# Expert up product with the weights as the stationary side, in a fused audio-tower block on one core

## The reference

```
scores = sigmoid(xf @ gate_w.T);  top_scores, top_idx = top_k(scores, 2)
buf[e, pos] = token                      # 64 experts, tokens sorted into slots
h = silu(buf @ w1[e]) * (buf @ w3[e])    # w1, w3: 128 x 64 for each expert
y = h @ w2[e]                            # w2: 64 x 128
out = shared(xf) + sum of the token's two y, each times its score + residual
```

## Time and profile before

| | |
|---|---|
| median of 3 runs | 320.98 us |
| profiled execution, its time | 321.12 us |
| profiled execution, its span | 319.3 us |
| TensorE: matmul records, busy | 2106, 197.5 us |
| VectorE busy | 214.1 us |
| GpSimd busy | 171.8 us |
| ScalarE busy | 61.9 us |
| granted TensorE clock, mean | 0.804 of 2.4 GHz |

### The profile page before, as it was taken

One profiled execution on the slowest core, in us unless ns is written; L12 is line 12 of the kernel. 1 busy time (PEld: TensorE's weight loads), 2 busy tenths in 40 slices (PEclk: granted clock), 3 DMA queues, 4 the chain that ended last, 5 costly groups with the idle time before them and its releaser, 6 DMA issues.

```text
span 319.3 us, 5301 instructions
## 1 busy us (share of the span) xinstructions
PE 197.5 (62%) x2106; PEld 159.1 (50%) x2106; DVE 214.1 (67%) x427; ACT 61.9 (19%) x167; POOL 171.8 (54%) x120
## 2 busy tenths in 40 slices
PE   0062828996767793894793694567277848989300
PEld 0052727874555573673582484442246727877200
DVE  0023986769899769989789859957839663374152
ACT  0033000020110110020020011011224752635300
POOL 2245776598669639669368676525205332003771
PEclk9999996999996859796598579755556796999755
DMA  8999999999953916565899100097810020824422
GB/s 280 241 383 364 418 423 418 417 418 418 397 200 113 359 56 233 213 232 205 268 218 225 49 0 20 25 200 211 225 38 10 8 66 18 233 68 117 115 62 72
DMA packets 32866, 64.14 MB, mean 201 GB/s; under 512 B 2858, under 2 KB 25351, under 8 KB 32391
## 3 DMA queue, kind: packets, MB, share of 16 engines
q1 hardware_dynamic: 30138, 59.17, 56.0%
q0 software_dynamic: 1024, 2.10, 2.3%
q10 hardware_dynamic: 1678, 2.52, 2.2%
HBM read 55.91 MB, written 7.86 MB: 200 GB/s over the span
## 4 chain that ended last, share of the span: by engine, by line
DVE 40%; PE 23%; DMA 15%; issue 8%; POOL 7%; ACT 3%; SPq 1%; POOLq 1%; DVEq 0%
PE bank L649 7%; DVE ring L957 7%; DMA mask<-in_L_tok_mask_dram 7%; DVE sc L987 6%; DMA ring<-in_L_tok_weight_dram 6%; DVE o L1000 5%; DVE prod L977 3%; POOL ring L453 3%; DVE prod L997 3%; DVE sc L979 3%; POOL rstd L373 2%; PE bank L690 2%; PE bank L780 2%; PE bank L805 2%; PE bank L790 2%
## 5 line engine op out<-in xcount | busy, mean ns | idle before, releaser
L384 POOL TENSOR_TENSOR ring<-ring,mask 128x896 f32<-128x896 f32 x48 | 104.9, 2202 | 22.4 <-DMA ring<-in_L_tok_weight_dram 22.2
L649 PE MATMUL bank<-ring,xT 128*64 128x128 f32 x1248 | 92.5, 312 | 39.5 <-POOL ring L384 27.5
L649 PEld LDWEIGHTS bank<-ring,xT 128*64 128x64 f32 x1248 | 82.9, 160 | 46.0 <-POOL ring L384 29.6
L957 DVE TENSOR_TENSOR ring<-ring,bank 128x1024 f32<-128x1024 f32 x24 | 29.1, 1214 | 31.2 <-ACT bank L474 18.3
L373 POOL TENSOR_TENSOR rstd<-mv,half 128x1 f32<-128x1 f32 (+1 forms) x24 | 18.3, 762 | 46.7 <-DVE mv L966 46.5
L404 POOL DMA_INDIRECT expert_inputs<-xf,scatter_index x16 | 21.8, 1365 | 35.0 <-DVE scatter_index L1065 32.6
L453 POOL DMA_INDIRECT ring<-expert_outputs,gather_index x16 | 16.0, 1000 | 26.8 <-DMA expert_outputs<-ring 22.2
L957 DVE TENSOR_TENSOR ring<-ring,mask 128x512 f32<-128x512 f32 x24 | 24.9, 1038 | 0.0
L987 DVE TENSOR_TENSOR sc<-sc,mx 128x16 f32<-128x16 f32 (+7 forms) x8 | 21.1, 2638 | 0.3
L1133 DVE TENSOR_TENSOR mask<-ring,bank 32x256 f32<-32x256 f32 (+1 forms) x24 | 10.0, 418 | 11.5 <-ACT ring L560 11.3
L780 PE MATMUL bank<-w,ring 128*64 128x128 f32 (+1 forms) x256 | 15.7, 305 | 1.5 <-DVE ring L1124 1.5
(11 more groups left out here) (137 smaller groups left out, 305.3 us busy)
## 6 DMA issues: line engine op xcount, KB each, us to landing
ring<-in_L_tok_weight_dram SPq DMA_DIRECT2D x48, 832.0 KB, 9.6
ring<-expert_inputs SPq DMA_DIRECT2D x6, 512.0 KB, 5.8
expert_outputs<-ring SPq DMA_DIRECT2D x12, 256.0 KB, 3.0
mask<-in_L_tok_mask_dram SPq DMA_DIRECT2D x3, 832.0 KB, 16.3
expert_inputs<-prod ACTq DMA_DIRECT2D x2, 1024.0 KB, 11.4
w2p<-in_L_ffn_w_dram SPq DMA_DIRECT2D x2, 1024.0 KB, 10.5
w<-in_x_dram SPq DMA_DIRECT2D x1, 1250.0 KB, 13.8
expert_inputs<-ring SPq DMA_DIRECT2D x1, 1024.0 KB, 12.5
```

Of the source, the lines that this page charges most:

```text
L384: pool.tensor_tensor(unit(j, q, SPLIT, UC), unit(j, q, SPLIT, UC), mask[:, (m + SPLIT) * D:(m + UC) * D], ALU.mult).then_inc(s_pmask, 1)
L649: last = pe.matmul(bank[j % 2][64 * par:64 * par + 64, 0:D], xT[:, (UC * t + c) * B:(UC * t + c + 1) * B], unit(j, 2 * t + par, c, c + 1), ...
L957: dve.tensor_tensor(both(j, t, a, b), both(j, t, a, b), m.rearrange("p (u f) -> p u f", u=1).to_broadcast([P, 2, (b - a) * D]), ALU.mult). ...
```

## The change

`up` swaps its sides. For each expert and each of `w1` and `w3` one matmul has the weight (128x64) as the stationary side and streams the expert's 64 or 32 slots. The result lies with the middle's 64 columns on the partitions: even experts on partitions 0 to 63, odd ones on 64 to 127, the slots along the free axis, `w1`'s product in columns 0 to 255 of the bank and `w3`'s in 256 to 511. That is the form in which `down` needs it. So `turn_mid`, `copy_midT`, the block-shaped tiles, their zeroing (four GpSimd memsets) and ScalarE's 0/1 multiplications (L558) are gone. `mid` is one 128x256 product on either engine. `down` now does one expert in a matmul, with 64 rows of the middle (partitions 0 to 63 or 64 to 127) against that expert's 64 rows of `w2`. The step of TensorE becomes `up(g)`, `turn_xs(g+2)`, `down(g-1)`, that of ScalarE `silu(g)`, `copy_y(g-1)`, `copy_xsT(g+2)`, and there is one step fewer. `down` writes to banks 7 and 3 in turn in all groups, where it used bank 7 alone for groups 0 to 7.

```diff
 def silu(g):                                  # ScalarE
     ...
     if g < STEPS_C:
-        for par in range(2):
-            act.activation(gt[g % 2][:, :, H * par:H * par + H], both[:, :, H:2 * H], ACT.Identity,
-                           scale=cst[:, C_PAR + par:C_PAR + par + 1])
-    act.activation(sil[g % 2], both[:, :, 0:H], ACT.Silu).then_inc(s_sil, 1)
+        act.copy(linear[g % 2], bank[U_BANK(g)][:, 256:512])
+    act.activation(gated[g % 2], bank[U_BANK(g)][:, 0:256], ACT.Silu).then_inc(s_sil, 1)
-def copy_midT(g):
     ...
 def up(g):                                    # TensorE
     ...
-    for l in range(count):
-        row, tile = l * slots % P, l * slots // P
-        last = pe.matmul(bank[U_BANK(g)][row:row + slots, tile * P:(tile + 1) * P],
-                         xsT[g % 2][:, l * slots:(l + 1) * slots],
-                         w13[:, first + l].rearrange("p a h -> p (a h)"), start=True, stop=True)
+    for n in range(count // 2):
+        for a in range(2):
+            for par in range(2):
+                l = 2 * n + par
+                last = pe.matmul(bank[U_BANK(g)][64 * par:64 * par + H, 256 * a + n * slots:256 * a + (n + 1) * slots],
+                                 w13[:, first + l, a], xsT[g % 2][:, l * slots:(l + 1) * slots], start=True, stop=True)
-def turn_mid(g):
     ...
 def down(g):
-    pe.wait_ge(s_hT, g + 1)
+    pe.wait_ge(s_hm, g + 1)
     ...
-    if g >= 1:
-        pe.wait_ge(s_ys, g if g <= GROUPS1 else g - 1)
-    if g == GROUPS1 + 1:
-        pe.wait_ge(s_flag, 1)
-    for n in range(count // 2):
-        row, tile = 2 * n * slots % P, 2 * n * slots // P
-        last = pe.matmul(bank[Y_BANK(g)][row:row + 2 * slots, tile * D:(tile + 1) * D],
-                         hT[g % 2][:, 2 * n * slots:2 * (n + 1) * slots], w2p[:, first // 2 + n, :],
-                         start=True, stop=True)
+    if g >= 2:
+        pe.wait_ge(s_ys, g - 1)
+    for l in range(count):
+        n, par = l // 2, l % 2
+        row, tile = l * slots % P, l * slots // P
+        last = pe.matmul(bank[Y_BANK(g)][row:row + slots, tile * D:(tile + 1) * D],
+                         midT[g % 2][64 * par:64 * par + H, n * slots:(n + 1) * slots],
+                         w2p[64 * par:64 * par + H, first // 2 + n, :], start=True, stop=True)
 def expert_steps(first, last):
     ...
             up(g)
-        if 1 <= g <= GROUPS:
-            turn_mid(g - 1)
-        if g >= 2:
-            down(g - 2)
         if g + 2 < GROUPS:
             turn_xs(g + 2)
+        if 1 <= g <= GROUPS:
+            down(g - 1)
 def mid(g):                                   # VectorE
-    for r in range(P // slots):
-        rows, half = slice(slots * r, slots * (r + 1)), r % 2 * H
-        last = dve.tensor_tensor(hm[MID_TILE(g)][rows, :, half:half + H], sil[g % 2][rows],
-                                 bank[U_BANK(g)][rows].rearrange("p (i f) -> p i f", f=2 * H)[:, :, H:2 * H], ALU.mult)
-    last.then_inc(s_hm, 1)
+    dve.tensor_tensor(midT[g % 2], gated[g % 2], bank[U_BANK(g)][:, 256:512], ALU.mult).then_inc(s_hm, 1)
 # GpSimd
-for i in range(4):
-    pool.memset(hm[2 + i], 0.0).then_inc(s_hmz, 1)
```

More of the change, by code:

```diff
@@ L200, in tower_kernel @@
         xsT = [ring_view(14336 + 512 * i, 512) for i in range(2)]
-        hT = [ring_view(15360 + 512 * i, 512) for i in range(2)]
-        sil = [ring_view(16384 + 256 * i, 256).rearrange("p (i h) -> p i h", h=H) for i in range(2)]
+        gated = [ring_view(15360 + 256 * i, 256) for i in range(2)]
+        linear = [ring_view(15872 + 256 * i, 256) for i in range(2)]
+        midT = [ring_view(16384 + 256 * i, 256) for i in range(2)]
         sw13 = ring_view(16896, 2 * D).rearrange("p (a d) -> p a d", a=2)
@@ L261, in tower_kernel @@
                                                  sem("shared_down"), sem("shared_added"))
[L262 to L265, removed]
+        s_t1, s_xsT, s_m1, s_sil, s_hm, s_m2, s_ys = (
+            sem("xs_transposed"), sem("xsT_copied"), sem("up"), sem("silu"), sem("mid"), sem("down"), sem("y_copied"))
         s_yout = [sem("y_out_1"), sem("y_out_2")]
@@ L425, in mid @@
                 if g >= 2:
[L426 to L429, removed]
+                    pool.wait_ge(s_m2, g - 1)
+                pool.tensor_tensor(midT[g % 2], gated[g % 2], linear[g % 2], ALU.mult).then_inc(s_hm, 1)
             pool.wait_ge(s_tok, 3 * NCH)
@@ L607, in _ @@
             copy_xfT(NCH - 1)
-            expert_steps(STEPS_C, GROUPS + 2)
+            expert_steps(STEPS_C, GROUPS + 1)
             silu_shared(1)
@@ L777, in up @@
                     pe.wait_ge(s_hm, g - 1)
-                for l in range(count):
-                    row, tile = l * slots % P, l * slots // P
-                    last = pe.matmul(bank[U_BANK(g)][row:row + slots, tile * P:(tile + 1) * P],
-                                     xsT[g % 2][:, l * slots:(l + 1) * slots],
-                                     w13[:, first + l].rearrange("p a h -> p (a h)"), start=True, stop=True)
-                last.then_inc(s_m1, 1)
-            def turn_mid(g):
-                pe.wait_ge(s_hm, g + 1)
-                if g >= 2:
-                    pe.wait_ge(s_hT, g - 1)
-                for i in range(PG):
-                    last = pe.transpose(bank[M_BANK(g)][:, i * P:(i + 1) * P], hm[MID_TILE(g)][:, i, :], ident)
-                last.then_inc(s_t2, 1)
+                for n in range(count // 2):
[4 more added lines that the diff above has]
+                                             w13[:, first + l, a], xsT[g % 2][:, l * slots:(l + 1) * slots], start=True, stop=True)
@@ L1166, in _ @@
             gather_slots(1, NCH1, NCH)
-            dve.wait_ge(s_hmz, 4)
             dve.wait_ge(s_hm, STEPS_C)
```

22 lines of the change are left out of this document (4 added, 18 removed).

## The result

The changed kernel took 330.0 us (328.2 to 332.1, 4 runs) against 321.5 (317.7 to 322.3, 4 runs): ratio 1.033, 95% interval 1.027 to 1.039. Slower, where 317.7 us was forecast. That is the result on record, but not all of it: run again untouched in later batches, on two chips, the same kernel took 316.8 and 315.8 us, 0.6% **less** than the kernel before.

The account below looks back on a forecast made before the run. Two paths end close together: group 7's store with the gathers (3.7 to 5.0 us earlier), and the shared expert with eight combines, ending last, 3.4 us earlier: 321.12 - 3.4 = 317.7 us; range 316 to 319.5, 8 in 10 314.7 to 322.

Parts of the forecast that it names:

- second path: Table 2's products, shared expert and eight combines: products end at 293.1, last combine 3.4 us earlier; this path ends last.
- What follows is unchanged: From the end of the products on, nothing changes: first combine at 306.0, last one at 310.6 instead of 314.06.
- Rival one: Gain dies at the end: hand-overs from TensorE some 3 us late beside gathers, 320.7 or 323.7 us; chance 0.24.
- (a): Around the last chunk's exponential: narrower GpSimd product, slots' transposes already done, ScalarE's table load earlier; -0.75 us.
- (b): Step 4, 4.7 us at a clock of 0.60: the 0.25 us saved per step counts as -0.4 us.
- (c): Steps 5 to 7 of TensorE: 0.25 us less each, -0.75 us together.
- (d): From step 8's up product to the copy of group 7's result: down product one step sooner, 3.7 against 5.52, -1.8 us.
- The store of group 7: Store behind group 7's copy took 4.29 us where the median is 3.0: up to 1.3 us more gain, by luck.
- rival four: More comes through: lateness gone, GpSimd's path ends last, clock may give another 1 us; 315 us, chance 0.10.
- GpSimd's path: Group 7's copy and store, then 16 gathers 1.30 us apart: ends 3.7 to 5.0 us earlier.
- Rivals two and three: Two: down product's row halves do not run together, 333 us, chance 0.08. Three: weight loads bind, 328 us, chance 0.04.

Follow-up runs that it names:

- before_again: The kernel before, run again untouched on chip C: 317.8 us.
- after_again: The changed kernel, run again untouched on chip C: 316.8 us, ratio 0.994 to the kernel before.
- b_plain: The kernel before plus 12 plain transfers of 128 rows from ScalarE's queue, three a step in steps 4 to 7, chip A: 318.3 us.
- held12: The changed kernel with GpSimd's gathers also waiting for the last group's down product, chip A: 324.2 us, ratio 1.013 to the kernel before.
- up12: The changed kernel with GpSimd's gathers waiting for the 12th (last group's) up product, chip B: 322.2 us, ratio 1.011 to the kernel before.

## Why the prediction was wrong

**The step that failed** is in the second path: "steps 8 and 9 take 3.6 each, step 10 3.0 ... 293.1", with every instruction of table 2 at its undisturbed rate beside gathers that now start 3.9 us earlier. In the first pair these parts took until 311.8, and the second path did not win 3.4 us but lost 8.5 (last combine 322.51 against 314.06). What failed is thus an overlap taken as free. In its place the runs show TensorE held back from 289.6 to 305.1 beside the gathers, and at the lower clock until 311.8; why it is held back stays open.

**Another error in the same path hid part of that.** "What follows is unchanged" kept the 12.9 us between the end of the products and the first combine (294.83 to 307.74), and the late signals of before are in these. Behind the stall it is 6.2 us (311.78 to 317.96), and 6.1 us on chip C (292.96 to 299.08). So the products ended 18.7 us after the forecast's 293.1, and the last combine only 11.9 us after its 310.6.

**Rival one had the place and not the size.** I had seen the lateness in the earlier trace rows and priced it as a delay of 3 us for each hand-over in the last group, 320.7 to 323.7 us, chance 0.24. It was the edge of something that holds back the instructions themselves. In the kernel before only the end of TensorE's work lay under the gathers, and the last combine waited for the last gather all the same: on chip C, without the lateness, it waits 1.87 us for it, against 1.68. From the scatter of the last chunk but one to the last combine it is 71.36 us with the lateness (242.70 to 314.06) and 71.23 without (239.67 to 310.90); the two traces' other difference, 3.0 us, lies ahead of that scatter. So the lateness cost the kernel before next to nothing, and its price could not be read there. The changed kernel starts its gathers with two `up` and three `down` products to go, and the 13th gather waits for them. An estimate of the worst was missing: a stall lasting as long as table 1's gathers, 12 x 1.30 = 15.6 us, laid on the path that I had forecast to end last, gives 317.7 + 15.6 = 333 us. That number could have been written down. It is no strict bound: the gaps last 15.5 us, but from `up` of group 10 to the end of the products it is 24.2 us against 7.1 on chip C, 17.1 more, and 2.6 of them lie behind the gaps, at the lower clock.

**How the sum stands without the stall.** On chip C both kernels were profiled, and the steps can be held against each other, in us at fixed points of before and after:

| point | before_again | after_again | difference |
|---|---|---|---|
| scatter of the last chunk but one | 239.67 | 240.00 | +0.33 |
| exponential's table load | 247.21 | 247.44 | +0.23 |
| `up` of group 4 | 262.08 | 262.20 | +0.12 |
| `up` of group 5 | 267.34 | 267.06 | -0.28 |
| `up` of group 8 | 277.76 | 278.71 | +0.95 |
| copy of group 7's result | 283.29 | 282.42 | -0.87 |
| first gather | 288.53 | 286.18 | -2.35 |
| last combine | 310.90 | 308.38 | -2.52 |

The lines that the readings below rest on, three of after_again, then one of before_again:

```profile
267.06 1.63 PE L754 MATMUL bank<-ring,w 128*64 128x64 f32 x32
...
272.70 0.66 PE L738 MATMUL bank<-cst,ring 128*128 128x128 f32 x4 [1.32 <-DMA ring<-expert_inputs]
...
308.38 0.35 DVE L1139 SCALAR_TENSOR_TENSOR ring<-ring,wts,hres 128x128 f32<-128x128 f32 x1 [1.85 <-DMA ring<-expert_outputs,gather_index]
...
310.90 0.35 DVE L1183 SCALAR_TENSOR_TENSOR ring<-ring,wts,hres 128x128 f32<-128x128 f32 x1 [1.87 <-DMA ring<-expert_outputs,gather_index]
```

- (a), the exponential, -0.75 forecast: -0.21 at `up` of group 4, counted from the scatter. Wrong in this pair. In the first pair the table load did come 0.8 us earlier against the scatter (247.94 - 240.49 = 7.45 against 250.97 - 242.70 = 8.27), but before_again has 7.54: what I read in the earlier trace rows was mostly that execution's own.
- (b), step 4, -0.4: -0.40. Right.
- (c), steps 5 to 7, -0.75: +1.23. Wrong, and this is a further step that failed. In step 6 the slots' transposes wait 1.32 us for the load of group 8's slots, which is chained to the last scatter; they stood behind `down` before, and the change puts them ahead of it, so a late load holds `down` as well. I had moved them in the sum and not asked what they wait for. Another 0.48 us went to a stretch partly at the lower clock in step 5 (`up` 1.63 us instead of 1.15, granted 0.67). Without the two it is -0.57.
- (d), -1.8: 282.42 - 278.71 = 3.71 against 283.29 - 277.76 = 5.53, so -1.82. Right.
- The store of group 7, "up to 1.3 more, as luck has it": from the copy's end to the first gather 3.17 us against 4.65, 1.5 less. The first pair has 3.16 against 5.17, so it was no luck; why it lands sooner was not tested.
- Which path ends last: GpSimd's, in both kernels, by 1.85 and 1.87 us of the last combine's wait. I had the second path last; rival four, GpSimd's path at 315 us, has it right and chips B and C agree with it (315.8, 316.8). That 317.7 lies near these too is luck: it was added up along a path that does not end last, with 6.7 us of late signals in it that these runs do not have.

**Rivals two and three are refuted on every chip.** Two halves of the array's rows run together: 16 records of `down` take 1.09 us, 0.06 us each, where one after another was to be 1.8. (That rival's price is also too high as added up: its 0.87 and 2.6 us a group are counted from the 0.89 of before, where the forecast has 1.03 in already.) The Trainium skill ("TensorEngine Tiling (Array Packing)", Gotcha 1) says that different row tiles cannot access the same PSUM bank at once; here they write to one bank, in different partitions, and no waiting is seen. And weight loads do not bind: 32 records of `up` in 1.15 us are 0.06 us a pair, as taken from the earlier trace rows, not 0.107.

## What to carry to other kernels

Where the profile shows signals of an engine arriving late under some traffic, take the length of that traffic as a first estimate of the worst price, add what a lower clock costs behind it, and ask what the change moves under it; that the present kernel does not suffer may only mean that its critical path is elsewhere. Of an operation that is moved ahead of another on the same queue, look up what it waits for, not only what it costs. And where a variant is free of a stall in another batch than the one that showed it, run the untouched kernel beside it before believing in a cure: an idle wait and 12 unused scatters looked like cures here.

## What the runs showed of the hardware

- **The same program takes 4 to 6% longer on one occasion than on another, and not every program does.** The changed kernel: 330.0 us, then 316.8 and 315.8. The kernel before with unused gathers: 337.1 and 317.9. The kernel before itself: 321.5 and 320.3 where gaps or late signals are seen, 318.1 to 318.4 elsewhere; the late signals do not explain that difference (above, and b_plain took 318.3 us with them). Chips B and C came up in two batches each and never showed it; chip A came up once, and the chip of the first pair is not known. Whether it is the chip or the hour stays open.
- **What holds TensorE back is open as well.** Where it happens it is beside gathers (plain transfers from ScalarE's queue on chip A left the steps at 2.94 us) and shows no releaser. Two plain causes can be set aside from the traces. The DMA engines are not busier: from 288 to 304 they are busy 24% of the time in the stalled trace and 47% on chip C. Nor does TensorE seem to wait for its program: of the queues that load instructions one packet starts at 289.28 and takes 0.88 us, the next starts at 308.66, behind the gaps. The bursts do not follow the gathers one by one either: six of them, from 293.70 to 300.89, begin 1.44 us apart, the gathers 1.30.
- **One sign points at the recording.** The kernel before has 2748 records of semaphore updates in the first trace and 3153 on chip C from the same program; the one with unused gathers 2833 on chip A and 3337 on chip B. Most of what is missing is missing beside gathers: from the start of the first real gather to the end of the last there are 81 such records in the first trace and 422 on chip C, beside the 12 unused gathers 57 on chip A and 314 on chip B. held12 lacks them too, though nothing in it is late (152, against 390 in up12 on chip B), and it runs on chip A. So the missing records go with the gathers and with chip A or the first pair, and whether it is they that hold the instructions back is not shown. The Trainium skill ("NOTIFIC — the notification-queue block", 7.1) says that the block which writes such records pushes back on their producers rather than lose one inside, which can stall an engine. By that the gaps would be the price of recording TensorE's instructions while something slows the records' way out. No run here tests it: every timed run has a recorded span and clock, so none was made without records, and 330 us may not be what the kernel takes unobserved.
